# Selective scan of a Perceiver layer: GpSimd takes nine of sixteen products with C and folds each of them to half its width

## The chip, the cores and the metric

The kernel runs on one core of a Trainium2 chip. The metric is the time of one execution in device microseconds. Five engines of the core run side by side, each with its own list of instructions in a fixed order: TensorE (PE in the profile, PEld its weight loads), VectorE (DVE), ScalarE (ACT), GpSimd (POOL) and SyncE (SP, which issues the transfers). They meet only at semaphores: an instruction waits until a count has been reached, and the instructions behind it on its engine wait with it.

## The reference

Two Perceiver layers run over a sequence of 128 positions of width 256. The stage that the change touches is the selective scan of the second layer, with 512 channels and 32 states per channel:

```
def step(h, inp):
    ut, dtt, Bt, Ct = inp
    dA = jnp.exp(dtt[..., None] * A)
    h = dA * h + dtt[..., None] * Bt[:, None, :] * ut[..., None]
    y = jnp.einsum('bdn,bn->bd', h, Ct)
    return (h, y)
...
return jnp.swapaxes(ys, 0, 1) + u * D
```

Each of the 512 x 32 states runs through 128 steps of a linear recurrence. The output of a channel is the sum over its 32 states of state times C. A gate, an output projection and a residual sum follow, and after them a mixture of eight experts, which is the last stage of the kernel.

## The kernel before, in words

The scan stage (`selective_scan`) lays channels on the 128 partitions, so there are four channel tiles, j = 0 to 3. The 32 states of a tile are cut into four quarters of eight states. A quarter is 8 x 128 = 1024 elements per partition, and there are sixteen of them, q = 0 to 15, with j = q // 4. For each quarter five things happen:

- ScalarE makes the decays, eight activations (L1683).
- TensorE makes the driving term in PSUM (`drive(q)`, L1822), two matmuls of 512 columns, each of which stands in the profile as two MATMUL instructions. It uses one of two PSUM slots, so `drive(q)` waits for the scan of q - 2.
- VectorE runs the recurrence over the quarter (L1764) and writes the states into the tile `h`.
- The product with C is made in place in `h`. VectorE makes it (L1769), or GpSimd (L1630) for the quarters that are listed in `POOL_READS`.
- TensorE sums the states with identity matmuls into one PSUM bank per tile (`add_up(q)`, L1837), again two matmuls of 512 columns, four MATMUL instructions. The bank holds four partial sums of 128 columns each.

TensorE's order is written out: `drive(q+2)`, then `add_up(q)`, then, after the first quarter of a tile, the transpose of the next tile's input (`turn`, L1813), and after the last quarter the projection of the tile before (`project`, L1846). `add_up(q)` waits for the product of q, and `drive(q+3)` stands behind it. VectorE's order is: the scan of q, its product if it is VectorE's, and then one of the small jobs: `step_size(j+1)` after the first quarter of a tile (six small instructions, L1732, L1735, L1738), a copy of the turned input after the second (L1742), and `total(j-1)` after the third (L1746, L1749), which folds the four partial sums and applies the gate. GpSimd has nothing but its products in this stretch.

VectorE's product L1769 and the small instructions L1732, L1735, L1738 and L1749 read two inputs from SBUF. The scan L1764 reads one from SBUF and one from PSUM. GpSimd's products read two from SBUF.

`Linker` (`link`) makes an engine wait for the end of its own instruction before the next one is started.

Of the kernel before, what the change touches and what calls it, by code (L numbers as in the profile page):

```python
# [5 lines left out]
ALU = mybir.AluOpType  # L6
# [1494 lines left out]
NS = 32  # L1501
# [32 lines left out]
QS = 8  # L1534
NQ = CT * NS // QS
LOG1P_SCALE = 0.005232676169910651
LOG1P = ((-1.00935769, 1.05169538), (0.08225224, 1.80484655), (1.42473666, 1.64380825), (2.32168775, 0.65757674))
POOL_READS = (1, 3, 5, 7, 9, 11, 13)


def selective_scan(nc, a, sb, sem, base, links, shared, ss, me):

    x, z, y, zT, ident, st, stats, rows, cols, ps = base
    vlink, alink, plink = links
    ip, op, xp, dp, cw, al = ss.ip, ss.op, ss.xp, ss.dp, ss.cw, ss.al
    with ExitStack() as own:
        def t(name, shape, dt=F32):
# [8 lines left out]
        bd, c_all = t("bd", [S, NS, S]), t("c_all", [P, NS, S])  # L1556
        decay = t("decay", [P, 2, NS, S])
        h = t("h", [P, 2, NS, S])
# [4 lines left out]
        E = {n: sem("ss_" + n) for n in ("consts_ready", "in_done", "tap_done", "conv_done", "tanh_ready", "u_ready", "zg_ready", "x_done", "x_copied",  # L1563
                                         "dt_done", "parts_ready", "raw_ready", "dt_ready", "du_ready", "c_passed",
                                         "c_loaded", "uD_ready", "bd_ready", "decay_ready", "driven", "scanned", "read", "pool_read",
                                         "summed", "tot_read", "y_ready")}
# [9 lines left out]
        def u_bank(j):  # L1576
            return ps[:, j, 0:S]
# [14 lines left out]
        def reads_before(q, pool):  # L1592

            return sum(1 for k in range(q + 1) if (k in POOL_READS) == pool)

        with nc.Block() as block:
# [10 lines left out]
            @block.gpsimd  # L1607
            def _(pool):
                for k, (root, _) in enumerate(LOG1P):
                    nc.gpsimd.memset(roots[:, k:k + 1], -root).then_inc(E["consts_ready"], 1)  # L1610
                nc.gpsimd.memset(decay[:, :, :, 0:1], 0.0).then_inc(E["consts_ready"], 1)
                pool.wait_ge(ss.loaded, SS_LOADED)
                nc.gpsimd.tensor_scalar(cwh[:, :, :], cw[:, :, :], 0.5, None, ALU.mult).then_inc(E["consts_ready"], 1)
                nc.gpsimd.tensor_scalar(cbh[:, :], cols[:, C_CONVB:C_CONVB + CT], 0.5, None, ALU.mult).then_inc(E["consts_ready"], 1)
                for j in range(CT):
                    pool.wait_ge(E["u_ready"], j + 1)
                    nc.gpsimd.tensor_scalar(uD[:, j, :], u[:, j, :], cols[:, C_DPAR + j:C_DPAR + j + 1], None, ALU.mult).then_inc(E["uD_ready"], 1)
                pool.wait_ge(E["x_copied"], 2)
                for q in range(NS // QS):
                    lo, hi = states(q)  # L1620
                    if q:
                        pool.wait_ge(E["du_ready"], 1)
                    nc.gpsimd.tensor_tensor(bd[:, lo:hi, :], ident[:, :].unsqueeze(1).to_broadcast([S, QS, S]),
                                            bT[:, lo:hi].unsqueeze(2).to_broadcast([S, QS, S]), ALU.mult).then_inc(E["bd_ready"], 1)
                for q in POOL_READS:
                    lo, hi = states(q)
                    hs = h[:, q // 4 % 2, lo:hi, :]
                    c_wait(pool, q)
                    pool.wait_ge(E["scanned"], q + 1)
                    nc.gpsimd.tensor_tensor(hs, hs, c_all[:, lo:hi, :], ALU.mult).then_inc(E["pool_read"], 1)  # L1630

            @block.scalar
            def _(act):
# [146 lines left out]
            @block.tensor  # L1780
            def _(pe):
                keep_warm(nc, pe, ps[:, 6, 0:P], ident, vlink.sem, chain + 1, chain + 18)
                pe.wait_ge(shared["z_ready"], 5)
                for c in range(DC):
                    mm = nc.tensor.transpose(zT_bank[:, c * S:(c + 1) * S], y[:, c * P:(c + 1) * P], ident[:, :])
                mm.then_inc(shared["zT_done"], 1)
                pe.wait_ge(shared["zT_ready"], 5)
                pe.wait_ge(ss.loaded, SS_LOADED)
                for j in range(2 * CT):
                    for c in range(DC):  # L1790
                        to = u_bank(j) if j < CT else z_bank[:, j - CT, :]
                        mm = nc.tensor.matmul(to, ip[:, c, j * P:(j + 1) * P], zT[:, c, :], start=(c == 0), stop=(c == DC - 1))
                    if j < CT or j == 2 * CT - 1:
                        mm.then_inc(E["in_done"], 1)
                for j in range(CT):
                    pe.wait_ge(E["u_ready"], j + 1)
                    mm = nc.tensor.matmul(dbl_bank, xp[:, j, :], u[:, j, :], start=(j == 0), stop=(j == CT - 1))
                mm.then_inc(E["x_done"], 1)
                for j in range(CT):
                    mm = nc.tensor.matmul(bT_bank, u[:, j, :], xp[:, j, RANK:RANK + NS], start=(j == 0), stop=(j == CT - 1))  # L1800
                mm.then_inc(E["x_done"], 1)
                pe.wait_ge(E["x_copied"], 2)
                for j in range(CT):
                    mm = nc.tensor.matmul(dt_bank(j), dp[:, j * P:(j + 1) * P], dbl[0:RANK, :], start=True, stop=True)
                    if j == 0 or j == CT - 1:
                        mm.then_inc(E["dt_done"], 1)
                keep_warm(nc, pe, ps[:, 3, 0:P], ident, E["parts_ready"], 1, PARTS)

                def turn(j):
                    pe.wait_ge(E["zg_ready"], 1)  # L1810
                    pe.wait_ge(E["du_ready"], j + 1)
                    pe.wait_ge(shared["turned_copied"], j + 2)
                    nc.tensor.transpose(ps[:, 4, j * S:(j + 1) * S], du[:, j, :], ident[:, :]).then_inc(shared["turned"], 1)  # L1813

                def drive(q):
                    j, (lo, hi) = q // 4, states(q)
                    pe.wait_ge(shared["turned_copied"], j + 3)
                    if j == 0:
                        pe.wait_ge(E["bd_ready"], q + 1)
                    at_least(pe, E["scanned"], q - 1)  # L1820
                    for k in range(2):
                        mm = nc.tensor.matmul(slot(q)[:, 512 * k:512 * k + 512], duT[:, j, :],  # L1822
                                              bd[:, lo + 4 * k:lo + 4 * k + 4, :].rearrange("p n s -> p (n s)"), start=True, stop=True)
                    mm.then_inc(E["driven"], 1)

                def add_up(q):
                    j, (lo, hi) = q // 4, states(q)
                    to = ps[:, 6 + j % 2, :]
                    if q % 4 == 0:
                        pe.wait_ge(E["raw_ready"], 1)  # L1830
                        at_least(pe, E["tot_read"], j - 1)
                    if q in POOL_READS:
                        pe.wait_ge(E["pool_read"], reads_before(q, True))
                    else:
                        pe.wait_ge(E["read"], reads_before(q, False))
                    for k in range(2):
                        mm = nc.tensor.matmul(to, ident[:, :], h[:, j % 2, lo + 4 * k:lo + 4 * k + 4, :].rearrange("p n s -> p (n s)"),  # L1837
                                              start=(lo == 0 and k == 0), stop=(hi == NS and k == 1), skip_group_check=True)
                        if lo == 0 and k == 0:
                            pe.wait_ge(E["uD_ready"], j + 1)  # L1840
                            nc.tensor.matmul(to[:, 0:S], ident[:, :], uD[:, j, :], start=False, stop=False, skip_group_check=True)
                    mm.then_inc(E["summed"], 1)

                def project(j):
                    pe.wait_ge(E["y_ready"], j + 1)
                    mm = nc.tensor.matmul(out_bank, ys[:, j, :], op[:, j, :], start=(j == 0), stop=(j == CT - 1))  # L1846
                    if j == CT - 1:
                        mm.then_inc(shared["out_done"], 1)

                turn(0)  # L1850
                drive(0)
                drive(1)
                for q in range(NQ):
                    j = q // 4
                    if q + 2 < NQ:
                        drive(q + 2)
                    add_up(q)
                    if q % 4 == 0 and j + 1 < CT:
                        turn(j + 1)
                    if q % 4 == 3 and j:  # L1860
                        project(j - 1)
                project(CT - 1)
# [277 lines left out]
```

## Time and profile before

| what | value |
|---|---|
| median of 3 runs | 1222.01 us (1221.83 to 1223.29) |
| the profiled execution, its own time | 1227.61 us |
| its span in the trace | 1225.9 us |
| busy: PE, DVE, ACT, POOL | 1157.2, 905.3, 898.8, 587.1 us |
| scan of the quarters in the trace | 1082.40 to about 1146.9 us |
| mixture of experts | from 1147.9 us to the end |

The span runs from the first to the last instruction of the profiled execution, and what lies around it is 1.7 us here. All durations below are from that one execution, which was 5.6 us longer than the median of the unprofiled runs. The timeline's columns are: start in us, duration in us, engine, line, operation, output and inputs, shapes, count of merged instructions, and in brackets the idle time before with what ended it. A merged row of n instructions gives the time from the first start to the last end.

### The profile page before, as it was taken

The page shows a single profiled execution, that of the slowest core. Times are in us where ns is not written, and L with a number is a line of the kernel's source. Part 1 is how long each engine was busy: PE and PEld are TensorE (multiplying, and loading weights), DVE is VectorE, ACT ScalarE, POOL GpSimd, SP SyncE. Part 2 cuts the span into 40 slices and gives each one's busy share as a digit, 9 for nine tenths or more (in the row PEclk, how much of TensorE's full clock was granted, in tenths as well). Part 3 has the DMA queues.
Part 4 walks back from the last instruction along what each step waited for, and adds up shares of the span by engine and source line. Part 5 has one row for each costly group of instructions (what it writes and reads, how often), then busy time and mean ns, then how long its engine had stood idle before and what let it go on. Part 6 is the DMA issues. An engine that isn't in the chain of part 4 may idle for free. (4 is left out here: it accounts for less than half of the span.)

```text
span 1225.9 us, 31791 instructions
## 1 busy us (share of the span) xinstructions
PE 1157.2 (94%) x12394; PEld 800.2 (65%) x12395; DVE 905.3 (74%) x1721; ACT 898.8 (73%) x1548; POOL 587.1 (48%) x548
## 2 busy tenths in 40 slices
PE   4899999999999999999999999999977979889898
PEld 2466666666666666666666666666656448744698
DVE  7677878887888888888787878787744569679632
ACT  4599988888888888888888888888841539386010
POOL 6165656565656565656565656565540420133000
PEclk8999999999999999999999999999989999989999
DMA  6364634444444444444444444444427674040274
GB/s 213 76 178 105 157 88 121 96 116 94 108 105 109 105 111 102 107 107 94 120 108 107 109 105 109 103 91 96 92 76 239 242 268 151 1 173 0 82 285 178
DMA packets 139186, 151.06 MB, mean 123 GB/s; under 512 B 17904, under 2 KB 126736, under 8 KB 139040
## 3 DMA queue, kind: packets, MB, share of 16 engines
q1 hardware_dynamic: 138496, 146.97, 44.5%
q8 instruction: 97, 1.59, 0.6%
q10 hardware_dynamic: 544, 2.10, 0.5%
q14 instruction: 49, 0.40, 0.1%
HBM read 72.25 MB, written 0.15 MB: 59 GB/s over the span
## 5 line engine op out<-in xcount | busy, mean ns | idle before, releaser
L456 POOL TENSOR_TENSOR pT_lo<-p_exp,pT_hi 128x896 f16<-128x896 f32 x223 | 420.6, 1886 | 323.8 <-ACT pT_hi L555 323.8
L536 ACT ACTIVATE p_exp<-ps,ln_k,esc 128x896 f32<-128x896 f32 x224 | 245.7, 1097 | 55.3 <-PE ps L897 47.4
L669 DVE TENSOR_REDUCE tile_max<-ps 128x128 f16<-128x896 f32 x224 | 244.4, 1091 | 49.9 <-PE ps L873 47.2
L555 ACT ACTIVATE pT_hi<-p_exp 128x896 f16<-128x896 f32 x224 | 211.7, 945 | 0.9
L664 DVE TENSOR_TENSOR v_lo<-ps,v_hi 128x512 f16<-128x512 f32 x196 | 135.5, 692 | 74.7 <-ACT v_hi L528 72.3
L860 PE MATMUL ps<-c_hi,wk_hi 128*128 128x448 f16 x448 | 159.3, 356 | 6.2 <-DVE c_lo L651 4.7
L915 PE MATMUL ps<-v_lo,pT_hi 128*128 128x64 f16 x1568 | 164.4, 193 | 0.0
L914 PE MATMUL ps<-v_hi,pT_hi 128*128 128x65 f16 x1568 | 164.3, 193 | 0.1
L916 PE MATMUL ps<-v_hi,pT_lo 128*128 128x65 f16 x1568 | 163.8, 193 | 0.0
L860 PE MATMUL ps<-c_hi,wk_lo 128*128 128x448 f16 x448 | 158.8, 354 | 0.0
L860 PE MATMUL ps<-c_lo,wk_hi 128*128 128x448 f16 x448 | 158.8, 354 | 0.0
L832 PE MATMUL ps<-wv_hi,c_hi 128*128 128x512 f16 x392 | 149.1, 380 | 0.0
L832 PE MATMUL ps<-wv_lo,c_hi 128*128 128x512 f16 x392 | 149.1, 380 | 0.0
L832 PE MATMUL ps<-wv_hi,c_lo 128*128 128x512 f16 x392 | 149.1, 380 | 0.0
L914 PEld LDWEIGHTS ps<-v_hi,pT_hi 128*128 128x128 f16 x1568 | 144.2, 97 | 0.3 <-POOL pT_lo L456 0.2
L915 PEld LDWEIGHTS ps<-v_lo,pT_hi 128*128 128x128 f16 x1568 | 142.9, 97 | 0.2
L916 PEld LDWEIGHTS ps<-v_hi,pT_lo 128*128 128x128 f16 x1568 | 143.0, 97 | 0.0
L684 DVE SCALAR_TENSOR_TENSOR k_rest<-ps,k_top 128x448 f16<-128x448 f32 x222 | 136.7, 616 | 3.3 <-ACT k_top L550 3.2
L873 PEld LDWEIGHTS ps<-q_hi,k_st 128*128 128x128 f16 x1568 | 106.4, 98 | 44.3 <-ACT p_exp L536 2.0
L528 ACT ACTIVATE v_hi<-ps 128x512 f16<-128x512 f32 x196 | 115.6, 590 | 21.1 <-PE ps L832 18.3
L873 PE MATMUL ps<-q_hi,k_st 128*128 128x128 f16 x1568 | 124.5, 219 | 3.4 <-ACT p_exp L536 3.4
L897 PE MATMUL ps<-q_low,k_st 128*128 128x128 f16 x1568 | 124.7, 219 | 2.2 <-ACT q_low L543 2.2
(350 smaller groups left out, 2074.8 us busy)
## 6 DMA issues: line engine op xcount, KB each, us to landing
k_st<-k_top SPq DMA_DIRECT2D x444, 112.0 KB, 2.3
k_st<-k_rest SPq DMA_DIRECT2D x444, 56.0 KB, 2.0
c_raw<-in_ctxT SPq DMA_DIRECT2D x14, 896.0 KB, 5.5
xa_ct<-in_ctxT SPq DMA_DIRECT2D x14, 896.0 KB, 6.3
xa_cn<-in_ctx SPq DMA_DIRECT2D x14, 896.0 KB, 7.5
me_w<-in_me_w SPq DMA_DIRECT2D x8, 1536.0 KB, 6.2
me_w<-in_me_w SPq DMA_DIRECT2D x8, 768.0 KB, 5.7
ss_c_all<-ss_bc SPq DMA_DIRECT2D x4, 512.0 KB, 5.9
```

The lines of the kernel that those rows point to most:

```text
L456: nc.gpsimd.tensor_tensor(pT_lo[:, n % 2, :, :].rearrange("p t s -> p (t s)"), p_exp[:, n % 2, :], pT_hi[:, n % 2, :, :].rearrange("p t s ...
L536: nc.scalar.activation(p_exp[:, n % 2, :], s_scores[n % 2], ACT.Exp, bias=ln_k[:, 0:1], scale=esc[:, n // H0 % 2:n // H0 % 2 + 1]).then_in ...
L555: nc.scalar.activation(pT_hi[:, n % 2, :, :].rearrange("p t s -> p (t s)"), p_exp[:, n % 2, :], ACT.Copy).then_inc(pT_hi_ready, 1)
L664: nc.vector.tensor_tensor(v_lo[:, tile, 8 * half:8 * half + 8, 0:DH], v_bank(vn).rearrange("p (h e) -> p h e", e=DH), v_hi[:, tile, 8 * ha ...
L669: nc.vector.tensor_reduce(tile_max[:, n % 2, :], s_scores[n % 2].rearrange("p (t s) -> p s t", s=S), AX.X, ALU.max).then_inc(tile_max_done, 1)
L684: nc.vector.scalar_tensor_tensor(out=k_rest[:, b, :], in0=k_bank(U), scalar=K_DOWN, in1=k_top[:, b, :], op0=ALU.mult, op1=ALU.subtract).th ...
L832: mm = nc.tensor.matmul(v_bank(vn), lhs, rhs, start=(k == 0), stop=(k == 5))
L860: mm = nc.tensor.matmul(k_bank(U), lhs, rhs, start=(k == 0), stop=(k == 5))
L873: mm = nc.tensor.matmul(s_scores[i][:, tile * S:(tile + 1) * S], k_st[:, n // 2 % 4, i, 0, tile * P:(tile + 1) * P], q_hi[:, h, :], start= ...
L914: nc.tensor.matmul(to, ph, v_hi[:, tile, h, 0:DH + 1], start=(tile == 0), stop=False)
L915: nc.tensor.matmul(to[:, 0:DH], ph, v_lo[:, tile, h, 0:DH], start=False, stop=False)
L916: mm = nc.tensor.matmul(to, pl, v_hi[:, tile, h, 0:DH + 1], start=False, stop=(tile == TILES - 1))
```

## The change

`POOL_READS` goes from seven to nine quarters. Quarters 6, 8 and 12 move from VectorE to GpSimd, and quarter 7 moves from GpSimd to VectorE. In each of GpSimd's quarters a second GpSimd instruction follows the product: it adds the upper four states onto the lower four, in place, 512 elements per partition. It is linked, so it waits for the product. `pool_read` is counted up by this second instruction. TensorE's `add_up` then takes only the lower half of such a quarter, with one matmul of 512 columns.

```
-POOL_READS = (1, 3, 5, 7, 9, 11, 13)
+POOL_READS = (1, 3, 5, 6, 8, 9, 11, 12, 13)
...
-                    nc.gpsimd.tensor_tensor(hs, hs, c_all[:, lo:hi, :], ALU.mult).then_inc(E["pool_read"], 1)
+                    link = plink.on(pool)
+                    link(nc.gpsimd.tensor_tensor(hs, hs, c_all[:, lo:hi, :], ALU.mult))
+                    lower = h[:, q // 4 % 2, lo:lo + QS // 2, :]
+                    nc.gpsimd.tensor_tensor(lower, lower, h[:, q // 4 % 2, lo + QS // 2:hi, :], ALU.add).then_inc(E["pool_read"], 1)
...
-                    for k in range(2):
+                    halves = 1 if q in POOL_READS else 2
+                    for k in range(halves):
                         mm = nc.tensor.matmul(to, ident[:, :], h[:, j % 2, lo + 4 * k:lo + 4 * k + 4, :].rearrange("p n s -> p (n s)"),
-                                              start=(lo == 0 and k == 0), stop=(hi == NS and k == 1), skip_group_check=True)
+                                              start=(lo == 0 and k == 0), stop=(hi == NS and k == halves - 1), skip_group_check=True)
```

On GpSimd, the end of its list for this stage, where L1630 is the product before and L1631 the same product now, with L1633 the new addition:

```order
-L1630 TENSOR_TENSOR ss_h<-ss_h,ss_c_all 128x1024 [waits ss_scanned,ss_c_loaded] x7
+L1631 TENSOR_TENSOR ss_h<-ss_h,ss_c_all 128x1024 [waits ss_scanned,ss_c_loaded]
+L1633 TENSOR_TENSOR ss_h<-ss_h 128x512 [waits pool_chain]
+L1631 TENSOR_TENSOR ss_h<-ss_h,ss_c_all 128x1024 [waits ss_scanned,ss_c_loaded]
+L1633 TENSOR_TENSOR ss_h<-ss_h 128x512 [waits pool_chain]
```

Seven products became nine pairs (the first two are shown), and each addition waits for its own product through GpSimd's chain semaphore.

On TensorE, quarters 8 to 11 as they are now, where L1825 is `drive`, L1841 the sum of the states, L1845 the term u times D, L1816 the transpose and L1850 the projection:

```order
+L1841 MATMUL ps<-ss_h,ident 128x512 [waits ss_pool_read,ss_tot_read,ss_raw_ready]
+L1845 MATMUL ps<-ss_uD,ident 128x128 [waits ss_uD_ready]
+L1816 MATMUL ps<-ident,ss_du 128x128 [waits turned_copied,ss_du_ready,ss_zg_ready]
+L1825 MATMUL ps<-ss_bd,ss_duT 128x512 [waits ss_scanned,turned_copied]
+L1825 MATMUL ps<-ss_bd,ss_duT 128x512
+L1841 MATMUL ps<-ss_h,ident 128x512 [waits ss_pool_read]
+L1825 MATMUL ps<-ss_bd,ss_duT 128x512 [waits ss_scanned,turned_copied]
+L1825 MATMUL ps<-ss_bd,ss_duT 128x512
```

The sum of quarter 8 now waits for `pool_read` and has lost its second matmul, and so has that of quarter 9. `drive(11)` and `drive(12)` stand behind them as before.

## Rows read from the trace of the kernel before

**Rows 1.** The page's first line: span and instructions.

```profile
span 1225.9 us, 31791 instructions
```

**Rows 2.** Windows over the scan, the experts and the stretch ahead of the scan.

```profile
core 0: us, PE busy (x) PEld busy (x) DVE busy (x) ACT busy (x) POOL busy (x), PEclk, DMA share, GB/s
1082.40:1146.90 64.50, 58.35 (x143) 25.04 (x141) 56.09 (x54) 38.75 (x133) 17.54 (x8) 1.00 0.12 45
1146.90:1225.90 79.00, 73.50 (x548) 69.29 (x548) 29.46 (x70) 7.90 (x13) 0.44 (x2) 0.99 0.60 211
...
1070.00:1080.00 10.00, 8.42 (x33) 6.89 (x34) 4.21 (x13) 5.47 (x19) 5.40 (x6) 0.57 0.53 156
```

**Rows 3.** Groups of the scan stretch: busy us, mean ns, then idle before.

```profile
L1764 DVE TENSOR_TENSOR_SCAN ss_h<-ss_decay,ps 128x1024 f32<-128x1024 f32 x16 | 36.3, 2277 | 5.1 <-PE ps L1822 4.1 <-issue 1.0
L1630 POOL TENSOR_TENSOR ss_h<-ss_h,ss_c_all 128x1024 f32<-128x1024 f32 x7 | 16.4, 2350 | 36.5 <-DVE ss_h L1764 36.5
L1769 DVE TENSOR_TENSOR ss_h<-ss_h,ss_c_all 128x1024 f32<-128x1024 f32 x9 | 11.3, 1258 | 0.9
```

**Rows 4.** Timeline of PE in the scan.

```profile
1092.89 1.98 PE L1837 MATMUL ps<-ss_h,ident 128*128 128x512 f32 x4 [0.74 <-POOL ss_h L1630]
1094.71 1.88 PE L1822 MATMUL ps<-ss_bd,ss_duT 128*128 128x512 f32 x4
...
1146.17 0.70 PE L1846 MATMUL ps<-ss_out_proj,ss_ys 128*128 128x256 f32 x2 [0.68 <-DVE ss_ys L1749]
```

**Rows 5.** Timeline of POOL in the scan.

```profile
1090.48 2.35 POOL L1630 TENSOR_TENSOR ss_h<-ss_h,ss_c_all 128x1024 f32<-128x1024 f32 x1 [6.99 <-DVE ss_h L1764]
...
1104.48 2.35 POOL L1630 TENSOR_TENSOR ss_h<-ss_h,ss_c_all 128x1024 f32<-128x1024 f32 x1 [5.87 <-DVE ss_h L1764]
1112.63 2.35 POOL L1630 TENSOR_TENSOR ss_h<-ss_h,ss_c_all 128x1024 f32<-128x1024 f32 x1 [5.79 <-DVE ss_h L1764]
```

**Rows 6.** Timeline of DVE in the scan.

```profile
1092.53 1.39 DVE L1769 TENSOR_TENSOR ss_h<-ss_h,ss_c_all 128x1024 f32<-128x1024 f32 x1
...
1096.70 2.29 DVE L1764 TENSOR_TENSOR_SCAN ss_h<-ss_decay,ps 128x1024 f32<-128x1024 f32 x1 [0.58 <-PE ps L1822]
1099.09 1.23 DVE L1769 TENSOR_TENSOR ss_h<-ss_h,ss_c_all 128x1024 f32<-128x1024 f32 x1
...
1102.06 2.28 DVE L1764 TENSOR_TENSOR_SCAN ss_h<-ss_decay,ps 128x1024 f32<-128x1024 f32 x1
...
1112.40 2.26 DVE L1764 TENSOR_TENSOR_SCAN ss_h<-ss_decay,ps 128x1024 f32<-128x1024 f32 x1
1114.76 1.29 DVE L1769 TENSOR_TENSOR ss_h<-ss_h,ss_c_all 128x1024 f32<-128x1024 f32 x1
...
1117.80 2.28 DVE L1764 TENSOR_TENSOR_SCAN ss_h<-ss_decay,ps 128x1024 f32<-128x1024 f32 x1
...
1125.91 4.46 DVE L1764 TENSOR_TENSOR_SCAN ss_h<-ss_decay,ps 128x1024 f32<-128x1024 f32 x2
...
1139.42 2.28 DVE L1764 TENSOR_TENSOR_SCAN ss_h<-ss_decay,ps 128x1024 f32<-128x1024 f32 x1
```

**Rows 7.** Timeline of a moment in the first cross attention, DVE and POOL.

```profile
77.85 1.89 POOL L456 TENSOR_TENSOR pT_lo<-p_exp,pT_hi 128x896 f16<-128x896 f32 x1 [1.07 <-ACT pT_hi L555]
...
79.14 1.08 DVE L651 SCALAR_TENSOR_TENSOR c_lo<-c_raw,c_scale,c_hi 128x448 f16<-128x448 f32 x1
...
79.71 0.67 POOL L447 TENSOR_SCALAR run_max<-m_col,esc 128x4 f32<-128x4 f16 x1
...
80.47 0.20 POOL L448 TENSOR_TENSOR drop<-run_max 128x4 f32<-128x4 f32 x1
```

**Rows 8.** Lines L447 and L651 over the run: ns minimum, median, maximum.

```profile
L447 POOL TENSOR_SCALAR run_max<-m_col,esc x56: 286/295/675, 64.0 to 905.9; 128x4 f32<-128x4 f16 x56
L651 DVE SCALAR_TENSOR_TENSOR c_lo<-c_raw,c_scale,c_hi x56: 678/1021/1102, 23.2 to 821.3; 128x448 f16<-128x448 f32 x56
```

**Rows 9.** Other two-input instructions of POOL, by form, over the whole run.

```profile
L456 POOL TENSOR_TENSOR pT_lo<-p_exp,pT_hi 128x896 f16<-128x896 f32 x223 | 420.6, 1886 | 323.8 <-ACT pT_hi L555 323.8
...
L463 POOL TENSOR_TENSOR wq<-acc,rec 128x256 f32<-128x256 f32 x3 | 1.8, 613 | 0.0
```

**Rows 10.** Timeline of ACT: the decays of the last tile.

```profile
1117.59 9.43 ACT L1683 ACTIVATE ss_decay<-ss_dt,ss_a_log 128x127 f32<-128x127 f32 x32 [4.25 <-DVE ss_dt L1735]
```

## The prediction, made before the changed kernel was run

> **What bounds the kernel now.** I read the span first [rows 1] and then the windows [rows 2]. The change works only inside the 64.5 us in which the quarters are scanned, 5% of the span. Whatever ends later there shifts the 79 us of experts as a block, since these start behind a barrier. In the scan TensorE is busy 58.35 of 64.5 us and VectorE 56.09, GpSimd 17.54. So two engines are nearly full and neither alone is the bound. The groups [rows 3] show why: a quarter costs TensorE a `drive` and an `add_up`, 1.72 us each (four instructions 0.43 us apart: the row of 1092.89 to that of 1094.71 is 1.82 with the 0.10 that the first instruction after a wait costs extra, and a row ends 0.16 after its last step [rows 4]). It costs VectorE a scan of 2.28 us and, where it has the product, 1.23 us more [rows 3, 6], plus about 1.8 us of `step_size` once a tile. The idle column names both directions: VectorE waited 4.1 us for `drive` [rows 3], and TensorE waited for a product of GpSimd [rows 4].
>
> The handovers are needed too. A product on VectorE starts 0.10 after its scan's end (1096.70 + 2.29 against 1099.09 [rows 6]). GpSimd starts 0.15 after the scan (1102.06 + 2.28 against 1104.48 [rows 5, 6]). TensorE starts 0.06 after GpSimd (1090.48 + 2.35 against 1092.89 [rows 4, 5]).
>
> **What VectorE and GpSimd do to each other.** VectorE's product takes 1.23 us, but 1.39 and 1.29 in two places. The first started at 1092.53 while GpSimd worked until 1092.83, and it ended at 1093.92, 1.09 after GpSimd's end. The second started at 1114.76, GpSimd ended at 1114.98, and it ended at 1116.05, 1.07 after [rows 5, 6]. So a VectorE instruction with two SBUF inputs makes no progress beyond its first 0.14 us until GpSimd's instruction is done. The scan is not touched: that of 1112.40 ran under GpSimd's product of 1112.63 and took 2.26 [rows 5, 6]. The reverse holds as well [rows 7]: VectorE's L651 was held up by GpSimd's L456 until 79.74 and then ran to 80.22, and GpSimd's next instruction, begun at 79.71, took 0.67 us where its median is 0.295 [rows 8]. It ended 0.16 after VectorE did. That is just the case the change makes nine times: a GpSimd instruction directly behind another, with a VectorE instruction waiting in between. It gets in, and GpSimd's second one is held.
>
> [...] The usual other guess, bandwidth shared in proportion, would give about +1.3 us below instead of +3.3.
>
> **The change part by part.**
>
> TensorE loses two of four summing instructions in nine quarters: 9 x 0.86 = 7.7 us of 58.35.
>
> VectorE gives away the products of 6, 8 and 12 and takes 7: 2 x 1.23 = 2.5 us less of 56.09.
>
> GpSimd gets two more products and nine additions of 512 elements. An addition of this shape is not in the trace. It lies between 0.61 us (256 elements) and 1.89 (896) [rows 9]. The straight line through the two f32 forms, 613 ns at 256 and 2350 at 1024, gives 613 + 256 x 2.262 = 1192 ns, and I take 1.19. The link before it costs 0.09: 79.71 + 0.67 to 80.47 [rows 7]. So a quarter occupies GpSimd for 2.35 + 0.09 + 1.19 = 3.63 us, nine of them 32.7 us. A quarter's sum becomes ready 1.28 us later than now, while `add_up` is 0.86 shorter: behind each GpSimd product `drive(q+3)` is 0.42 us later if it waits at all.
>
> The Trainium skill (GPSIMD Engine Reference, 3.1) gives 4497 ns for a 2048-element f32 addition. An estimate from that page is a quarter of it, 1.12 us, and the walk below would then end at +2.8.
>
> I walk the three engines in program order with these times. The starts of scans are the milestones [rows 6].
>
> To scan 4: GpSimd's product 1 runs 1090.48 to 1092.83. VectorE's product 2 waits since 1092.67 and takes the ports until 1093.92. GpSimd's addition then needs its last 1.06: 1094.98. `add_up(1)` starts 1095.03, needs 0.96, `drive(4)` starts 1095.99, needs 1.88, and scan 4 starts at 1097.97. It was 1096.70 [rows 6]: +1.3.
>
> To scan 5 nothing changes (5.35 us of VectorE work): 1103.31, +1.3.
>
> To scan 8: product 6 has left VectorE, but GpSimd does 5 and 6 back to back, 1105.74 to 1109.37 and 1109.39 to 1113.06. VectorE reaches product 7 at 1111.86, when GpSimd's addition 6 is just beginning, and is held until 1113.06. Scan 8 starts at 1114.06 instead of 1112.40: 10.75 against 10.34 us, +0.4.
>
> To scan 9: scan 8 ends, GpSimd begins product 8 at 1116.49, and `step_size(3)`, six small two-input instructions, gets one in ahead of it. The second waits for the product's end at about 1118.8, then the addition takes 1118.9 to 1120.12, and the rest ends at 1121.2. Now: 1112.40 to 1117.80, 5.40 with a VectorE product inside. Then: 7.14. This is +1.7, the largest term.
>
> To scan 11: VectorE's present wait for the turned input is gone, but addition 9 is held behind product 10 until 1128.26, and the gate instruction of `total(1)` is held behind addition 9. Scan 11 starts at 1128.37, 7.17 against 8.11: -0.9.
>
> To scan 15: GpSimd does 11, 12 and 13 back to back from 1130.80. Addition 13 is held by product 14 (until 1141.54) and ends at 1142.60; the gate instruction of `total(2)` waits for it. Scan 15 starts at 1142.71, 14.34 against 13.51: +0.8.
>
> From scan 15 to the end both have 7.5 us (1139.42 to 1146.87 [rows 4, 6]).
>
> The sum is 1.3 + 0.4 + 1.7 - 0.9 + 0.8 = +3.3 us. ScalarE stays hidden: the last tile's decays begin behind `step_size(3)`, at about 1121.2, and take 9.4 us [rows 10], done at 1130.6, ahead of scan 15 and each a good 2 us ahead of its scan. No transfer is touched.
>
> Against its own execution this is 1225.9 + 3.3 = 1229.2 us of span. Against the median it is 1222.0 + 3.3 = **1225.3 us**, 0.27% more. A difference under 0.2%, 2.4 us, can't be told from none in this kernel.
>
> The walk has one near tie: VectorE's product 7 and GpSimd's addition 6 ask for the ports within about 0.01 us. If VectorE wins, scan 8 and `step_size(3)` come earlier and the end is +2.3. The walk's path goes through eight additions, so each 0.1 us on their price moves the end by 0.8: 1.5 us per addition would give +5.8.
>
> **Rivals.**
>
> *The near tie goes the other way:* +2.3, 1224.3. Chance 0.12, half of it under 2.4 us.
>
> *Collisions cost half* (each engine slowed, none stopped): halfway between the walk and the same walk without any collision. Without collisions, scan 4 starts at 1097.09, scan 8 at 1111.94, scan 9 at 1115.95, scan 15 at 1138.67, the end at -0.7. So +1.3, 1223.3, or with no collisions 1221.3. For it speaks only that two engines' records can be placed 0.1 us wrong; against it speak rows 7 and 8. Chance 0.19 together, split 0.13 and 0.06.
>
> *TensorE's relief comes through, the kernel is faster:* the addition costs only 0.61 us as the 256-element row, and VectorE's products do not meet it. The path without collisions has four additions in it, 4 x 0.58 less: -2.9, 1219.1. It takes an addition under about 0.75 us for this to show. The slope of rows 3 and 9 speaks against it. Chance 0.06.
>
> *Dear additions:* 1.89 us as the 896-element row, 8 x 0.70 more than the walk: +8.9, 1230.9. Reading both inputs from one tile in place is nothing the rows have. Chance 0.05.
>
> *TensorE's clock falls:* its busy time in the scan drops from 58.4 to 50.6 us. The clock is 1.00 there and was 0.57 at 1070 to 1080, between the two levels of 1.2 and 2.4 GHz, after a stretch of short matmuls with waits [rows 2]. Ten us at the lower level would double about 8 us of work, +4 and more as part of it is hidden. Its new gaps are under 2 us. Chance 0.03.
>
> **How the numbers follow.** The walk has 0.55 and by itself 1224.3 to 1226.5 (addition of 1.07 to 1.35 us). Slower by over 0.2%: 0.55 + 0.06 + 0.05 + 0.03 = 0.69. Within 0.2%: 0.06 + 0.19 = 0.25. Faster: 0.06. The range leaves out the fast case, the case without collisions and the dear additions, 0.17: 1222.3 to 1228.2. Its upper end takes in an addition of 1.5 us (+5.8).
>
> **What would show it.** In the profile after: the line of the addition with a shortest time near 1.19 us and a longest above 2 (held by a VectorE product); GpSimd near 32.7 us plus about 3 of being held; VectorE's mean product well above 1.26 us, product 7 above 2; small instructions of L1735 (the new number of L1732) of over 1 us where `step_size(3)` stands; TensorE's busy time in the scan near 51 us with waits for GpSimd of 1 to 3 us; the scan ending near 1150. The prediction is wrong if the shortest addition is far from 1.19, if no VectorE instruction is longer than before, or if `step_size(3)` slips in ahead of the product of 8 as a whole.

## The result, and the profile after

The change made the kernel slower: median 1232.22 us of four runs (1230.44 to 1232.9) against 1222.65 us (1221.83 to 1223.37), ratio 1.0067 with a 95% interval of 1.0049 to 1.0084, so +8.2 us, between +6.0 and +10.3; the two medians lie 9.6 us apart. The forecast was +3.3. The direction was right and the size too small: less than half.

The page of the profiled execution begins with this line, which answers to [rows 1]:

```profile
span 1228.7 us, 31765 instructions
```

The two profiled spans differ by only 2.8 us, and that is not the size of the change: the whole programs ahead of the scan differ by some us from one execution to the next. What can be compared exactly is the scan stretch itself, from the start of the first scan to VectorE's residual sum. It was 64.51 us before (1082.40 to 1146.91). Here are its windows after, then the two-us windows in which the granted clock falls; they answer to [rows 2]:

```profile
core 0: us, PE busy (x) PEld busy (x) DVE busy (x) ACT busy (x) POOL busy (x), PEclk, DMA share, GB/s
1078.14:1149.76 71.62, 56.26 (x125) 23.30 (x123) 58.14 (x52) 38.77 (x133) 36.52 (x19) 0.93 0.12 45
1088.00:1090.00 2.00, 0.00 (x0) 0.00 (x0) 1.90 (x3) 2.00 (x9) 1.92 (x2) 1.00 0.00 0
1090.00:1092.00 2.00, 1.16 (x2) 0.64 (x3) 1.86 (x1) 2.00 (x9) 0.79 (x1) 0.78 0.00 0
1092.00:1094.00 2.00, 2.00 (x3) 0.68 (x2) 0.00 (x0) 2.00 (x9) 1.99 (x1) 0.50 0.00 0
1124.00:1126.00 2.00, 1.11 (x2) 0.64 (x3) 1.97 (x3) 2.00 (x9) 0.83 (x1) 0.81 0.00 0
1126.00:1128.00 2.00, 2.00 (x3) 0.68 (x2) 1.18 (x1) 0.94 (x4) 0.68 (x1) 0.50 0.00 0
1144.00:1146.00 2.00, 1.13 (x3) 0.56 (x4) 0.82 (x1) 0.00 (x0) 0.00 (x0) 0.93 0.00 0
1146.00:1148.00 2.00, 2.00 (x4) 0.94 (x3) 0.12 (x1) 0.00 (x0) 0.00 (x0) 0.50 0.00 0
```

The stretch is 71.62 us, 7.1 longer than before, which lies inside the interval of the ratio. Its mean clock is 0.93 where it was 1.00: three times TensorE's clock went to its lower level, 1.2 instead of 2.4 GHz. Each time TensorE had just waited 2.5 to 3 us (it was busy for 0.00 of the 2 us from 1088.00).

TensorE's timeline after shows what that costs; it answers to [rows 4]:

```profile
1085.94 1.95 PE L1825 MATMUL ps<-ss_bd,ss_duT 128*128 128x512 f32 x4 [1.36 <-DVE ss_h L1767]
1090.84 1.85 PE L1841 MATMUL ps<-ss_h,ident 128*128 128x512 f32 x2 [2.95 <-POOL ss_h L1633]
1092.48 2.90 PE L1825 MATMUL ps<-ss_bd,ss_duT 128*128 128x512 f32 x4
...
1124.88 1.76 PE L1841 MATMUL ps<-ss_h,ident 128*128 128x512 f32 x2 [2.78 <-POOL ss_h L1633]
1126.43 2.99 PE L1825 MATMUL ps<-ss_bd,ss_duT 128*128 128x512 f32 x4
...
1144.87 2.97 PE L1841 MATMUL ps<-ss_h,ident 128*128 128x512 f32 x4 [2.47 <-DVE ss_h L1772]
```

`add_up(1)` waited 2.95 us for GpSimd's addition, and then it took 1.85 us for its two instructions, where 1.12 is the time at the full clock after a wait, and the `drive` behind it took 2.90 instead of 1.88. The same happens at quarter 9, and at quarter 15, where the wait is for VectorE and the four instructions of the sum take 2.97 us; behind a wait at the full clock such a row is 1.98 us long [rows 4].

GpSimd's and VectorE's rows, in the order of time, show the collisions that the walk, the prediction's table of starts, had counted; they answer to [rows 5, 6]. "Ports" stands for the access to SBUF that the two engines have to take in turn:

```profile
1086.23 2.35 POOL L1631 TENSOR_TENSOR ss_h<-ss_h,ss_c_all 128x1024 f32<-128x1024 f32 x1 [6.98 <-DVE ss_h L1767]
1088.66 2.13 POOL L1633 TENSOR_TENSOR ss_h<-ss_h 128x512 f32<-128x512 f32 x1
...
1109.42 2.35 POOL L1633 TENSOR_TENSOR ss_h<-ss_h 128x512 f32<-128x512 f32 x1
1112.99 2.35 POOL L1631 TENSOR_TENSOR ss_h<-ss_h,ss_c_all 128x1024 f32<-128x1024 f32 x1 [1.22 <-DVE ss_h L1767]
1115.42 1.27 POOL L1633 TENSOR_TENSOR ss_h<-ss_h 128x512 f32<-128x512 f32 x1
```

```profile
1088.27 1.39 DVE L1772 TENSOR_TENSOR ss_h<-ss_h,ss_c_all 128x1024 f32<-128x1024 f32 x1
...
1095.49 2.29 DVE L1767 TENSOR_TENSOR_SCAN ss_h<-ss_decay,ps 128x1024 f32<-128x1024 f32 x1 [3.63 <-PE ps L1825]
...
1109.42 1.23 DVE L1772 TENSOR_TENSOR ss_h<-ss_h,ss_c_all 128x1024 f32<-128x1024 f32 x1
1110.57 2.28 DVE L1767 TENSOR_TENSOR_SCAN ss_h<-ss_decay,ps 128x1024 f32<-128x1024 f32 x1
1112.77 0.27 DVE L1735 SCALAR_TENSOR_TENSOR ss_prod<-ss_sq,ss_e 128x128 f32<-128x128 f32 x1
1113.06 4.09 DVE L1735 SCALAR_TENSOR_TENSOR ss_prod<-ss_sq,ss_prod 128x128 f32<-128x128 f32 x3
...
1117.72 2.28 DVE L1767 TENSOR_TENSOR_SCAN ss_h<-ss_decay,ps 128x1024 f32<-128x1024 f32 x1
```

Addition 1 began at 1088.66 and took 2.13 us, because VectorE's product of 1088.27 held the ports until 1089.66; the addition ended 1.13 us after that. `step_size(3)` got one small instruction done at 1112.77, and its next three took 4.09 us instead of 0.95, across GpSimd's product and addition of quarter 8. And the near tie at quarter 7 went to VectorE: its product of 1109.42 took the plain 1.23 us, and GpSimd's addition 6, started at the same time, took 2.35.

The line of the addition over the run, ns minimum, median and maximum:

```profile
L1633 POOL TENSOR_TENSOR ss_h<-ss_h x9: 1261/1266/2348, 1088.7 to 1138.0; 128x512 f32<-128x512 f32 x9
```

**Where the 7.1 us come from**, with all starts counted from the first scan's. Before, scan 4 started at 14.3, scan 8 at 30.0, scan 9 at 35.4, scan 11 at 43.5, scan 15 at 57.0 and the end was 64.5 [rows 6]. After, they are 17.35, 32.4, 39.6, 46.8, 63.1 and 71.6. The walk had 15.6, 31.7, 38.8, 46.0, 60.3 and 67.8. From scan 8 to 9 the walk has 7.14 us and the trace 7.15, and from scan 9 to 11 they have 7.17 and 7.18. To scan 4 the trace has 1.8 more, from 11 to 15 2.0 more, and in the tail 1.1 more: in these three pieces lie the three stretches of the lower clock. From scan 4 to 8 it has 1.0 less: the near tie. So 3.3 - 1.0 + 4.8 = 7.1. That the 4.8 us are the clock's is at this point only a matter of where they lie; the first experiment tests it.

### The profile page after: what moved, and what is told of

Its sections match the earlier page's. It is cut to its first block and busy times, and to the rows that moved or that the text cites. A ratio compares the mean times of both kernels' runs of the same rounds, so it can differ in the third digit from the quotient of the medians.

```text
span 1228.7 us, 31765 instructions
## 1 busy us (share of the span) xinstructions
PE 1151.5 (94%) x12377; PEld 794.4 (65%) x12377; DVE 907.5 (74%) x1719; ACT 898.8 (73%) x1548; POOL 606.1 (49%) x559
```

## The experiments

All compare with the kernel before on the same chip. Theory A: the port collisions and late sums cost what the walk says, and the rest is TensorE's clock, which goes to its lower level (I call this a fall) after waits that the change makes. Theory B: collisions and lateness are all of it. The scan stretch is read from each profile, since times of whole executions scatter by several us. Of most kernels only the window of the stretch is shown.

### Idle matmuls in TensorE's long waits

```
+FILL = {1: 10, 5: 6, 6: 6, 9: 10, 15: 8}
...
+                    for _ in range(FILL.get(q, 0)):
+                        nc.tensor.matmul(ps[:, 5, 2 * P:3 * P], ident[:, :], ident[:, :], start=True, stop=True, skip_group_check=True)
```

> The changed kernel with idle matmuls of 128 columns on TensorE into an unused part of a PSUM bank, ahead of the sums of quarters 1, 5, 6, 9 and 15 (10, 6, 6, 10 and 8 of them, about 0.21 us each), so that TensorE works through most of its waits; nothing else differs. Theory A (the missing 6 us are TensorE's clock, which fell to its lower level after three waits of 2.5 to 2.9 us): the granted clock is 1.00 through the whole scan, and the time falls by about 5 us against the changed kernel, to 1226 to 1228 us. Theory B (the ports and the late sums make all of it, the clock is a bystander): no change, 1231 to 1233 us, or a little more where an idle matmul delays a sum.

Measured: median 1228.06 us, ratio 1.0034 (1.0020 to 1.0049). The window of its scan stretch:

```profile
1080.96:1148.54 67.58, 60.06 (x205) 31.25 (x203) 57.70 (x52) 38.49 (x132) 37.12 (x19) 1.00 0.10 40
```

The clock is 1.00 throughout and the stretch is 4.0 us shorter than that of the changed kernel, although TensorE does 40 matmuls more. Theory B, which has no place for this, falls. The time of the whole execution is at the upper edge of what was expected.

The idle matmuls have a cost of their own at quarter 15, as TensorE's timeline shows:

```profile
1143.03 1.95 PE L1841 MATMUL ps<-ident 128*128 128x128 f32 x16
1144.81 1.88 PE L1848 MATMUL ps<-ss_h,ident 128*128 128x512 f32 x4
```

VectorE's last product was done at 1143.96, and without them the sum would have started 0.05 us later, as in the kernel before; it started 0.8 us after that, less 0.1 us that the first instruction after a wait costs extra. The last piece, from scan 15 to the end, is 8.17 us against 7.49 before. Taking these 0.7 us off leaves 66.9 us, and the walk with the near tie lost has 66.8. So nearly all of the 4.8 us belongs to the falls and what they set off. Scan 4 starts 1.70 us earlier than in the changed kernel (15.65 against 17.35 after the first scan), and from scan 11 to 15 the filled kernel needs 14.34 us, as the walk says, against 16.31.

### The moved products alone

```
                     nc.gpsimd.tensor_tensor(hs, hs, c_all[:, lo:hi, :], ALU.mult).then_inc(E["pool_read"], 1)
...
-                    halves = 1 if q in POOL_READS else 2
+                    halves = 2
```

> The changed kernel without the additions: the products of 1, 3, 5, 6, 8, 9, 11, 12 and 13 are GpSimd's, and TensorE sums both halves of each quarter. The walk over the three engines with the ports as an exclusive lock gives +1.3 us against the kernel before, no TensorE wait above 1.2 us. Theory A and the walk: 1223 to 1225 us, clock 1.00 in the scan. Theory B with the moved products as the main cause: 1227 us or more.

Measured: 1225.47 us, ratio 1.0019 (1.0005 to 1.0032). The window of its stretch:

```profile
1081.13:1146.86 65.73, 58.50 (x143) 25.06 (x141) 57.35 (x52) 38.75 (x133) 22.22 (x10) 1.00 0.12 45
```

The stretch grew by 1.22 us where the walk said 1.3. Taking two products from VectorE on balance (three given away, one taken back) made the kernel slower by itself. TensorE's longest waits are 1.35 and 1.36 us, a little over the 1.2 expected.

### The additions alone

```
-POOL_READS = (1, 3, 5, 6, 8, 9, 11, 12, 13)
+POOL_READS = (1, 3, 5, 7, 9, 11, 13)
```

> The split of before (1, 3, 5, 7, 9, 11, 13 on GpSimd), but each of these seven products is followed by the addition, and TensorE sums half a quarter. The walk without any loss of clock gives +3.7 us, with TensorE waits of about 3.1, 1.9, 2.7 and 2.8 us for quarters 1, 5, 7 and 11. Theory A: three falls of the clock on top, at about 1.7 us each, +8 to +9, 1230 to 1232 us. Theory B (clock a bystander): +3.7, 1226 to 1227 us.

Measured: 1230.23 us, ratio 1.0056 (1.0038 to 1.0074). The window of its stretch, then three sums of TensorE's timeline:

```profile
1079.00:1149.15 70.15, 54.41 (x129) 22.90 (x127) 57.93 (x55) 38.59 (x133) 28.80 (x15) 0.98 0.12 44
```

```profile
1091.70 1.64 PE L1848 MATMUL ps<-ss_h,ident 128*128 128x512 f32 x2 [2.95 <-POOL ss_h L1638]
...
1116.78 1.12 PE L1848 MATMUL ps<-ss_h,ident 128*128 128x512 f32 x2 [2.62 <-POOL ss_h L1638]
...
1133.82 1.12 PE L1848 MATMUL ps<-ss_h,ident 128*128 128x512 f32 x2 [2.65 <-POOL ss_h L1638]
```

+5.6 us in the stretch: more than the walk's 3.7, less than with three falls, and near the walk with one fall of 1.7 (5.4). The clock fell after the first of the long waits, but not after those of 2.62 and 2.65 us, behind which the sum took 1.12 us as at the full clock. So my rule "a wait of 2.5 us or more, a fall" was too simple: a long wait makes a fall possible, not certain.

### One addition, with and without idle matmuls

The kernel before, with the addition of quarter 1 alone (`FOLDS = (1,)`), and the same with ten idle matmuls ahead of that sum (`FILL = {1: 10}`).

> The kernel before with one single addition, that of quarter 1. It is held behind VectorE's product 2, and TensorE waits about 3.1 us for it. The walk without a loss of clock: +1.3 us. Theory A: one fall of the clock in the scan, of 1.7 us, on top: +3.0, 1225 to 1226 us, and the granted clock goes to its lower level within 2 us of the wait's end. Theory B: +1.3, 1223 to 1224.5 us.

> The partner of e4_fold_q1 (the kernel before plus the addition of quarter 1 alone), now with ten idle matmuls ahead of the sum of quarter 1, which fit into TensorE's wait of 3.1 us. Theory A: no fall of the clock in the scan, stretch at the walk's 64.51 + 1.29 = 65.8 us, 1.75 less than its partner's 67.55. Theory B (the clock is not what costs): 67.5 again.

Measured: 1226.79 us, ratio 1.0028 (1.0016 to 1.0040), and 1225.54 us, ratio 1.0019 (1.0007 to 1.0030). These intervals overlap; what tells the two apart is one trace of each. TensorE's timeline of the first, then of the second:

```profile
1091.61 1.99 PE L1848 MATMUL ps<-ss_h,ident 128*128 128x512 f32 x2 [2.94 <-POOL ss_h L1638]
1093.40 2.75 PE L1830 MATMUL ps<-ss_bd,ss_duT 128*128 128x512 f32 x4
```

```profile
1090.07 2.39 PE L1841 MATMUL ps<-ident 128*128 128x128 f32 x20
1093.18 1.13 PE L1848 MATMUL ps<-ss_h,ident 128*128 128x512 f32 x2 [0.72 <-POOL ss_h L1638]
1094.14 1.88 PE L1830 MATMUL ps<-ss_bd,ss_duT 128*128 128x512 f32 x4
```

The sum is ready equally late in both. In the first, sum and `drive` run at the lower clock; in the second they don't. The stretches are 67.55 and 65.86 us, +3.04 and +1.35; +3.0 and +1.3 had been expected with and without a fall. One fall costs 1.69 us here, and the two kernels differ in nothing but the ten idle matmuls.

### Idle matmuls at quarter 1 only

`FILL = {1: 10}` in the changed kernel.

> The changed kernel with ten idle matmuls ahead of the sum of quarter 1 only. Theory A (each long wait is followed by one fall of TensorE's clock that costs about 1.7 us where TensorE is needed): the fall at quarter 1 is gone, that at quarter 9 and that at the end stay, 1.7 us less than the changed kernel, scan stretch near 70 us instead of 71.6. Theory B (one of the three waits carries all of it, or the clock falls at random): either the whole 4 us is gone, scan near 67.6, or nothing, 71.6.

Measured: 1227.99 us, ratio 1.0041 (1.0025 to 1.0057), stretch 68.09 us. It met neither expectation: 3.5 us less than the changed kernel, where theory A had 1.7 and the rival all 4 or nothing. The sum of quarter 9 now waited 0.75 us at full clock, because one fall, the only one left, came earlier, behind the wait of quarter 6. Its row of TensorE's timeline, then the windows of two us around it:

```profile
1109.92 1.12 PE L1848 MATMUL ps<-ss_h,ident 128*128 128x512 f32 x2 [1.96 <-POOL ss_h L1638]
```

```profile
1110.00:1112.00 2.00, 2.00 (x4) 0.93 (x5) 1.97 (x3) 0.22 (x1) 0.92 (x1) 0.81 0.00 0
1112.00:1114.00 2.00, 2.00 (x4) 0.75 (x3) 1.97 (x2) 0.00 (x0) 1.92 (x2) 0.50 0.00 0
```

So a wait of 1.96 us can bring a fall too. In the changed kernel the same wait of the same sum (1111.83, also 1.96 us) brought none. What decides it is not shown; a rule by the length of the wait alone does not hold. This one fall cost about 1.2 us: from the first scan to scan 11 this kernel took 46.27 us and the filled one 45.07.

The fall at quarter 15 went for another reason. Its wait is short here:

```profile
1142.20 1.98 PE L1848 MATMUL ps<-ss_h,ident 128*128 128x512 f32 x4 [0.83 <-DVE ss_h L1777]
```

In the changed kernel the fall at quarter 9 had delayed scan 12 by 1.70 us, the order in which GpSimd's addition 13 and VectorE's product 14 took the ports turned round, that product took 2.01 us instead of 1.23, and TensorE then waited 2.47 us for product 15. So, as far as these traces show, the third fall followed from what the second one had shifted.

### The changed kernel again

> The changed kernel once more, unchanged, for a second trace of it and more times beside the kernel before. If the falls of TensorE's clock belong to its long waits, this trace shows two or three of them in the scan again, after waits of 2.5 us or more, not always after the same ones, and the scan stretch is about 66.8 us plus 1.6 to 1.75 for each. Median 8 to 9 us over the kernel before.

Measured: median 1232.92 us of six runs, ratio 1.0064 (1.0043 to 1.0085). Its second trace has the same three falls behind the same waits and the same stretch, at another place in the execution:

```profile
1080.93:1152.55 71.62, 56.26 (x125) 23.30 (x123) 58.14 (x53) 38.76 (x133) 36.53 (x19) 0.93 0.12 45
```

The waits are 2.94, 2.78 and 2.47 us. The expectation that the falls would not always come after the same waits was not met, so they are not random from one execution to the next, as far as two traces show. The wait at quarter 15 is not one of GpSimd's: TensorE waits 2.47 us for VectorE's last product, and in the kernel before its wait at that place was 1.13 us.

### A second GpSimd instruction that reads, and one that doesn't

Both have the split of before, TensorE sums everything, and idle matmuls ahead of the sums of 1, 5, 7, 11 and 15 keep the clock up. So GpSimd's second instruction is pure lateness. They differ in one line:

```
+                    nc.gpsimd.tensor_tensor(scratch[:, 0:512], scratch[:, 0:512], scratch[:, 512:1024], ALU.add).then_inc(E["pool_read"], 1)
```
```
+                    nc.gpsimd.memset(scratch[:, 0:1264], 0.0).then_inc(E["pool_read"], 1)
```

> A pair with g2_scratch_set, both with the split of before, with TensorE summing both halves of every quarter, and with idle matmuls ahead of the sums of 1, 5, 7, 11 and 15 that keep the clock up. Here each of GpSimd's seven products is followed by an addition of 512 elements inside a scratch tile, so its result is used by nobody. The walk with the ports as an exclusive lock: +6.5 us against before. VectorE's products and small two-input instructions are stretched where they meet it. If ports don't matter, this kernel and its partner take the same time.

> The partner: the same, but GpSimd's second instruction is a memset of 1264 elements of the scratch tile, which takes about as long (967 ns for 1040 elements in the trace before, so an estimate of 1.17 us) and reads nothing. Port theory: it neither holds VectorE's two-input instructions nor is held by them, +4.9 us, 1.6 us less than its partner, and every memset takes the same time. Rival (any GpSimd instruction holds VectorE, or lateness alone counts): equal to its partner within 0.3 us.

Measured: 1230.91 us, ratio 1.0055 (1.0036 to 1.0074), and 1231.42 us, ratio 1.0049 (1.0032 to 1.0065). The times of whole executions don't tell them apart. The profiles do. The window of the stretch of the first, then of the second:

```profile
1079.32:1150.45 71.13, 67.02 (x227) 35.04 (x225) 57.01 (x54) 38.78 (x133) 29.16 (x15) 1.00 0.11 41
```

```profile
1080.83:1150.45 69.62, 66.47 (x227) 34.97 (x225) 55.93 (x54) 38.87 (x134) 25.74 (x15) 1.00 0.11 41
```

GpSimd's second instruction in the groups by line (busy us, mean ns of one, idle before), of the first, then of the second:

```profile
L1639 POOL TENSOR_TENSOR ss_scratch<-ss_scratch 128x512 f32<-128x512 f32 x7 | 11.6, 1653 | 0.6
```

```profile
L1639 POOL MEMSET ss_scratch<- 128x1264 f32 x7 | 8.1, 1152 | 0.4
```

The stretches are +6.6 and +5.1 against the walk's +6.5 and +4.9, and their difference is 1.5 us where 1.6 was expected. The addition takes 1.27 us alone and 1.65 on average, since VectorE's two-input instructions hold it three times (2.25, 2.13 and 2.13 us); the memset is never held, nor does it hold VectorE. About 0.1 us per instruction of the difference is that the memset is shorter than the addition (1.15 against 1.27). So GpSimd's instruction that reads SBUF collides and the one that only writes does not; one with a single input was not tried here. The Trainium skill (SBUF — State Buffer, section "SBUF: two separate sides") has the rule that a VectorE instruction with two SBUF inputs is in conflict only with a GpSimd instruction that reads SBUF; these two kernels agree with it. That VectorE and GpSimd exclude each other rather than share is shown by the ends: in the changed kernel addition 1, 1.26 us when alone, ended 1.13 us after VectorE's product, and VectorE's product 14, 1.23 us when alone, ended 1.08 us after GpSimd's addition 13.

### Another split, and a warm start

The walk, used the other way round, looks for the split that ends first: products of 1, 3, 5, 7, 9, 12, 13 and 14 on GpSimd, additions for 3 and 13 alone.

```
+POOL_READS = (1, 3, 5, 7, 9, 12, 13, 14)
+FOLDS = (3, 13)
```

> Another split, found with the same walk: GpSimd has the products of 1, 3, 5, 7, 9, 12, 13 and 14, and only 3 and 13 are followed by the addition. No TensorE wait above 1.2 us. The walk gives -1.7 us against the kernel before, scan stretch 62.8 us, granted clock 1.00, median 1221 to 1222.5 us. If the walk only fits what it was fitted to, the stretch comes out more than 1 us off.

Measured: 1222.00 us against 1223.74, ratio 0.9980 (0.9969 to 0.9991): faster than the kernel before. The stretch was expected at 62.8 us and is 62.89, 1.6 less than before:

```profile
1077.36:1140.25 62.89, 56.89 (x139) 24.21 (x137) 56.06 (x53) 38.78 (x133) 22.40 (x11) 1.00 0.13 51
```

The last kernel adds idle matmuls ahead of the scan, such as these:

```
                 for j in range(CT):
+                    for _ in range(3):
+                        nc.tensor.matmul(ps[:, 5, 2 * P:3 * P], ident[:, :], ident[:, :], start=True, stop=True, skip_group_check=True)
                     pe.wait_ge(E["u_ready"], j + 1)
```

> The split of f2_split (products of 1, 3, 5, 7, 9, 12, 13, 14 on GpSimd, additions for 3 and 13), and idle matmuls on TensorE ahead of the scan too, three before each product with x_proj, three before the wait for its copy, and twice as many in the loop that keeps the clock up: in every trace so far the clock is at its lower level for 7 to 10 us right ahead of the first scan. If it stays up there, the first driving terms take 1.72 us each instead of about 3.4, so up to 3 us less than f2_split, 1218 to 1221 us, 0.3 to 0.4% under the kernel before. If the idle matmuls only delay what stands behind them, the same as f2_split or up to 2 us more.

Measured: 1221.55 us against 1223.39, ratio 0.9992 (0.9979 to 1.0004), which can't be told from the kernel before nor from the split without them. The expected 1218 to 1221 us was missed. The stretch of this trace is 62.93 us, so the split's gain inside the scan repeats, while its gain in whole executions, 0.2% in one comparison, is not confirmed by this second one. The windows ahead of the scan, first of the split alone, then with the idle matmuls:

```profile
1070.00:1075.00 5.00, 4.30 (x16) 3.09 (x15) 2.59 (x8) 4.34 (x15) 3.14 (x3) 0.50 0.87 254
1075.00:1080.00 5.00, 4.17 (x9) 1.62 (x8) 2.53 (x2) 4.93 (x18) 3.47 (x2) 0.83 1.02 373
```

```profile
1070.00:1075.00 5.00, 4.45 (x26) 3.26 (x27) 2.52 (x8) 4.36 (x16) 2.81 (x2) 1.00 1.01 317
1075.00:1080.00 5.00, 4.17 (x11) 1.70 (x10) 4.54 (x6) 5.00 (x19) 2.79 (x2) 1.00 1.02 375
```

The clock stays up as intended. From the stage's first VectorE instruction to the first scan it took 22.0 us instead of 22.8 (1053.27 to 1075.25 and 1054.58 to 1077.36), a gain of 0.8 us and not 3, since most of that time is VectorE's and ScalarE's chain. Whether these 0.8 us hold over many runs stays open.

## Why the prediction was right and wrong

**The ports, right.** VectorE's two-input instructions and GpSimd's reading ones exclude each other in these kernels, both ways, and an instruction of VectorE gets in between GpSimd's product and its addition. The scan 8 to scan 9 piece, the largest term, came out at 7.15 us against 7.14, and the two scratch kernels show the cause apart. GpSimd's 36.5 us busy fit the announced 32.7 and about 3 of being held.

**The price of an addition**, 1.19 us from a straight line, is 1.26 us. By the walk's 0.8 us per 0.1 that would be 0.6 too little. The traces show only about 0.1 of it: scan 4 starts 15.65 us after the first where the first wait is filled and the walk has 15.57, and the later pieces up to scan 15 agree with the walk, the near tie allowed for, to 0.01 us.

**The near tie**, named as a rival with 0.12, went the other way: -1.0, seen in product 7's 1.23 us. The walk could not have known: it had the two requests within 0.01 us.

**TensorE's relief**, 7.7 us of work, was rightly booked as worth nothing by itself: the additions alone cost 5.6 us in the stretch, and the one on quarter 1 alone cost 1.35 without a fall (65.86 against 64.51) for 0.86 us of TensorE's work saved. TensorE's busy time in the scan fell only to 56.3 us and not to about 51, since its work at the lower clock takes longer. (The rival that let the relief come through has a slip of 0.1 us: 4 x 0.58 off the -0.7 gives -3.0, not -2.9.)

**The step that failed is the last rival:** "TensorE's clock falls ... Its new gaps are under 2 us. Chance 0.03." The walk itself contradicted the sentence. [Rows 4] have `drive(3)` done at 1092.15 (the start of 1092.89 less the wait of 0.74), nothing in the change moves it, and the walk starts `add_up(1)` at 1095.03: a gap of 2.9 us. Another of nearly 3 lies ahead of `add_up(9)`, whose addition the walk ends at 1128.26. The ends of the chain were worked out, and the gaps between them were not read. The trace has 2.95 and 2.78 us, then a lower clock, and with the third fall, which the walk had no gap for (it follows from the second), 4.8 of the 7.1 us of the stretch. The one-addition pair shows 1.69 us for one fall, and filling the gaps gave 4.0 us back, 4.7 without the delay that the filling itself makes. The price was mis-sized too, "ten us at the lower level ... +4 and more" as one event: it is three short ones, of 1.7, 1.7 and 1.1 us, and 0.3 for product 14. That the sum is still "+4 and more" is luck: the rival named the right effect, gave it 0.03, and had another event in mind.

The range, up to +6.2 us over the median of before, was therefore too short, though it took in a dear addition. With the tie lost and three falls the same working gives +7.1.

**What stays open:** why the waits of 2.62 and 2.65 us in the kernel with the additions alone brought no fall, while one of 1.96 us did in another. And the difference of the medians, 9.6 us on four runs and 9.5 on the later six, is 2.4 us more than that of the stretches. The stretch before had 79.0 us behind it, that after 78.9, so it doesn't lie behind the scan. The estimates of the ratio, +8.2 and +7.8 us, are nearer than the medians, and their intervals reach down to +5.3 and take 7.1 in. The scatter of whole executions of one kernel goes with their mean granted clock: of the 23 runs of the kernel before that were taken with the repeat of the changed kernel, those up to 1223.4 us have 0.986 or 0.987 and those above 1225 us have 0.983. The profiled execution of the kernel before has 0.983 with 1.00 in the scan, so in it at least the lower clock lies outside the scan. It was not settled further.

## What to carry to other kernels

When a wait of TensorE is moved or made longer, list the gaps that your own time table leaves on it, not only the end of the chain: waits of 2 to 3 us in this full stretch cost up to another 1.7 us each through the clock, though not every one did. A few idle matmuls in the gap are a cheap test and a cheap cure, as long as they end before the wait does: those that overran cost 0.7 us. A delay from one fall can open the gap for the next, so look at the new gaps again. Handing two-input elementwise work to GpSimd beside a busy VectorE is not free even if GpSimd is idle: here each such instruction shut out VectorE's two-input instructions for its whole length, and was shut out by them, while the scans, which have an operand in PSUM, ran beside it untouched (2.27 to 2.29 us each). So place it under those. A hand-made table of starts is worth its work: it forecast the stretches of three other kernels (65.73, 65.86 and 62.89 us) to about 0.1 us and found the faster split, and it missed what it had no column for.

## What was not expected of the hardware

The clock fell after waits of 1.96, 2.47, 2.78 and 2.95 us, and stayed up after waits of 2.62 and 2.65 us in another kernel and after one of 1.96 in the changed kernel itself. Two executions of the same kernel, 2.8 us apart in the place of the scan, had their falls at the same three waits and the same stretch to 0.01 us. A GpSimd addition inside one tile, in place, takes 1.26 us for 512 elements, 6% over the straight line through the other two-input instructions.
